# Attention totals spread by a transfer instead of GpSimd, and full tiles for the leftover rows of the last expert layer

## The reference

```
# L1 and L3 attention, per batch entry and head (L1: 4 heads, L3: 16), 1024 queries, 1024 + 154 keys, 64 wide
dots = jnp.einsum('bhid,bhjd->bhij', q, k) * scale
attn = jax.nn.softmax(dots, axis=-1)
out = jnp.einsum('bhij,bhjd->bhid', attn, v)
return out.transpose(0, 2, 1, 3).reshape(b, n, h * d) @ Wo + bo

# L3 experts: 2048 tokens, 32 experts, 4 per token, each expert takes at most cap = 320 tokens
xe = xp[buf_tok].reshape(E, cap, DIM)
h = jax.nn.silu(jnp.einsum('ecd,edh->ech', xe, w1)) * jnp.einsum('ecd,edh->ech', xe, w3)
out = jnp.einsum('ech,ehd->ecd', h, w2) * buf_w.reshape(E, cap, 1)
y = jnp.zeros((N + 1, DIM), x.dtype).at[buf_tok].add(out.reshape(E * cap, DIM))[:N]
```

## Time and profile before

| | |
|---|---|
| median of 3 runs | 3232.53 us (3228.24 to 3237.84) |
| the profiled execution's own time | 3235.65 us |
| its span | 3233.9 us |
| TensorE busy | 2877.3 us, 89% of the span |
| weight loads busy | 2129.0 us, 66% |
| VectorE busy | 1891.3 us, 58% |
| ScalarE busy | 1430.9 us, 44% |
| GpSimd busy | 658.2 us, 20% |

### The profile page before, as it was taken

One profiled execution on the slowest core, in us unless ns is written; L12 is line 12 of the kernel. 1 busy time (PEld: TensorE's weight loads), 2 busy tenths in 40 slices (PEclk: granted clock), 3 DMA queues, 4 the chain that ended last, 5 costly groups with the idle time before them and its releaser, 6 DMA issues. The chain is left out here.

```text
span 3233.9 us, 46916 instructions
## 1 busy us (share of the span) xinstructions
PE 2877.3 (89%) x14020; PEld 2129.0 (66%) x14021; DVE 1891.3 (58%) x3602; ACT 1430.9 (44%) x2987; POOL 658.2 (20%) x736
## 2 busy tenths in 40 slices
PE   6796789975998889999689999999999999579997
PEld 4795455534887678999556766766676666355664
DVE  4414465505555444434488888888888888273333
ACT  1232534431211115444447777777777777321110
POOL 0133001111442110000201111111111111106776
PEclk8797889995999779999799999999999999789999
DMA  1342010002322010000010101110100010036776
GB/s 40 122 150 86 2 27 15 15 1 90 101 95 92 15 40 27 26 13 0 17 29 17 23 15 30 22 23 15 23 21 17 23 24 8 1 70 159 164 159 140
DMA packets 147165, 158.11 MB, mean 49 GB/s; under 512 B 36816, under 2 KB 121702, under 8 KB 146726
## 3 DMA queue, kind: packets, MB, share of 16 engines
q1 hardware_dynamic: 109318, 94.41, 10.6%
q0 software_dynamic: 21280, 37.93, 5.4%
q10 hardware_dynamic: 16416, 24.12, 2.2%
HBM read 105.77 MB, written 29.84 MB: 42 GB/s over the span
## 5 line engine op out<-in xcount | busy, mean ns | idle before, releaser
L2035 ACT ACTIVATE l3a_pt_hi<-l3a_banks 128x512 fp32r<-128x512 f32 (+2 forms) x640 | 382.4, 598 | 314.3 <-PE l3a_banks L1976 257.0
L2146 DVE TENSOR_TENSOR l3a_pt_lo<-l3a_pt,l3a_pt_hi 128x512 fp32r<-128x512 f32 (+2 forms) x640 | 462.2, 728 | 81.0 <-ACT l3a_pt L2036 76.6
L2036 ACT ACTIVATE l3a_pt<-l3a_banks 128x512 f32<-128x512 f32 (+2 forms) x640 | 378.1, 591 | 0.0
L2116 DVE TENSOR_REDUCE l3a_maxima<-l3a_banks 128x1 f32<-128x1178 f32 x256 | 351.0, 1373 | 3.5 <-PE l3a_banks L1923 3.3
L1976 PE MATMUL l3a_banks<-l3a_pt_hi,l3a_v 128*65 128x512 f32 (+2 forms) x640 | 287.0, 448 | 12.1 <-ACT l3a_out L2050 12.1
L1989 PE MATMUL l3a_banks<-l3a_q,l3a_k 128*128 128x512 f32 (+2 forms) x640 | 254.5, 398 | 6.4 <-ACT l3a_pt L2036 4.9
L1990 PE MATMUL l3a_banks<-l3a_q,l3a_k 72*128 72x512 f32 (+5 forms) x640 | 253.5, 396 | 0.0
L1976 PE MATMUL l3a_banks<-l3a_pt_lo,l3a_v 128*65 128x512 f32 (+2 forms) x640 | 252.9, 395 | 0.0
L1976 PE MATMUL l3a_banks<-l3a_pt_hi,l3a_v_lo 128*65 128x512 f32 (+2 forms) x640 | 252.8, 395 | 0.0
L1923 PE MATMUL l3a_banks<-l3a_k,l3a_q 128*128 128x512 f32 (+1 forms) x768 | 207.8, 379 | 7.7 <-DVE l3a_maxima L2116 7.6
L2174 POOL PARTITION_BROADCAST l3a_shared<-l3a_inverse x65 | 62.6, 963 | 595.7 <-issue 595.7
(11 more groups left out here) (584 smaller groups left out, 6056.2 us busy)
## 6 DMA issues: line engine op xcount, KB each, us to landing
l3f_w<-in_L_ffn_w SPq DMA_DIRECT2D x96, 256.0 KB, 3.6
l0f_w<-in_L_ffn_W ACTq DMA_DIRECT2D x12, 1024.0 KB, 6.7
l1f_w<-in_L_ffn_W ACTq DMA_DIRECT2D x18, 512.0 KB, 4.5
l2f_w<-in_L_ffn_w SPq DMA_DIRECT2D x16, 512.0 KB, 4.6
l3a_q<-l3a_q SPq DMA_DIRECT2D x64, 128.0 KB, 2.3
l3a_k<-l3a_k SPq DMA_DIRECT2D x64, 128.0 KB, 2.3
l0f_w<-in_L_ffn_W SPq DMA_DIRECT2D x4, 1024.0 KB, 7.3
l1f_w<-in_L_ffn_W SPq DMA_DIRECT2D x6, 512.0 KB, 5.9
```

The lines of the kernel that those rows point to most:

```text
L2035: act.activation(a.pt_hi[0:rows, n % a.pt_slots, :], a.st_bank[0:rows, n % 2, :], ACT.Exp, bias=bias, scale=scale)
L2036: act.activation(a.pt[0:rows, n % 4, :], a.st_bank[0:rows, n % 2, :], ACT.Exp, bias=bias, scale=scale).then_inc(a.exped, 1)
L2116: dve.tensor_reduce(a.maxima[:, n:n + 1], banks.rearrange("p a b -> p (a b)")[:, 0:KEYS], AX.X, ALU.max).then_inc(a.maxed, 1)
L2146: dve.tensor_tensor(a.pt_lo[0:rows, slot, :], a.pt[0:rows, n % 4, :], a.pt_hi[0:rows, slot, :].bitcast(F32), ALU.subtract).then_inc(a.lo_m ...
```

## The change

1. In L1 and L3 attention `partition_broadcast` is gone. A third transfer of SP spreads the inverted row to 64 partitions, into a tile `shared` that has now two buffers, by the group's parity. GpSimd only multiplies. SP no longer waits for GpSimd's broadcast before it moves the inverses back, but waits until the spread has landed before it goes on.
2. In the L3 expert loop both rests of a pair are turned at once, as full 128 x 128 transposes, with the rows of the pair's first expert (6 transposes there, 4 for the second). `xt` holds a pair: columns 0 to 319 for the first expert, with its rest at the end, 320 to 639 for the second, with its rest at the start. The rest's product in `p_y` takes 72 columns of `hidden` instead of 64: the 8 added ones are spare zeros for the first expert, and columns of the next piece for the second; their results are not read.

```diff
 def move_totals(sp, a, k, g):
     sp.wait_ge(a.o_kept, k + 1)
     sp.dma_start(a.totals[:], a.out[HEAD:HEAD + 1, g % 2, :]).then_inc(a.moved, 16)
     sp.wait_ge(a.inverted, k + 1)
-    sp.wait_ge(a.spread_done, k + 1)
     sp.dma_start(a.inverse[:], a.totals[:]).then_inc(a.returned, 16)
     sp.wait_ge(a.returned, k * 16 + 16)
+    sp.dma_start(a.shared[:, g % 2, :], a.inverse[:].unsqueeze(1).to_broadcast([1, HEAD, BLOCK])).then_inc(a.spread_out[g % 2], 16)
+    sp.wait_ge(a.spread_out[g % 2], spread_count(k, g))
     sp.sem_inc(a.row_returned, 1)
...
     pool.wait_ge(a.ot_done, k + 2)
-    pool.wait_ge(a.returned, k * 16 + 16)
     pool.sem_inc(a.passed, 1)
-    pool.partition_broadcast(a.shared[0:HEAD, :], a.inverse[:], channels=HEAD).then_inc(a.spread_done, 1)
-    pool.wait_ge(a.spread_done, k + 2)
-    pool.sem_inc(a.passed, 1)
+    pool.wait_ge(a.spread_out[g % 2], spread_count(k, g))
     b, (hi, _) = g // 2, head_rows(g % 2)
-    pool.tensor_tensor(a.out_t[hi, parity, b * BLOCK:(b + 1) * BLOCK], a.out[0:HEAD, g % 2, :], a.shared[0:HEAD, :],
+    pool.tensor_tensor(a.out_t[hi, parity, b * BLOCK:(b + 1) * BLOCK], a.out[0:HEAD, g % 2, :], a.shared[:, g % 2, :],
                        ALU.mult).then_inc(a.ot_done, 1)
...
+    WIDE = REST + 8
+    IN_HIDDEN = ((0, P, 2 * P), (REST, REST + P, 0))
...
             def turn_rows(e, u, i):
                 pe.wait_ge(x_loaded[u], i * (16 * WHOLE) + 16 * WHOLE)
-                pe.wait_ge(rest_kept, i + 1)
-                pe.sem_inc(passed, 1)
+                if u == 0:
+                    pe.wait_ge(rest_kept, i + 1)
+                    pe.sem_inc(passed, 1)
                 pe.wait_ge(xt_kept, e * DC + 1)
-                rest = slice(u * REST, (u + 1) * REST)
                 for c in range(DC):
                     for j, (at, n) in enumerate(PIECES[0:WHOLE]):
-                        pe.transpose(p_xt[:, c, at:at + n], x_rows[:, u, j, c * P:(c + 1) * P], chip.ident[:])
-                    at, n = PIECES[WHOLE]
-                    ins = pe.transpose(p_xt[:, c, at:at + n], rest_tile[rest, c * P:(c + 1) * P], chip.ident[rest, rest])
+                        ins = pe.transpose(p_xt[:, c, at:at + n], x_rows[:, u, j, c * P:(c + 1) * P], chip.ident[:])
+                    if u == 0:
+                        ins = pe.transpose(p_xt[:, c, 2 * P:3 * P], rest_tile[:, c * P:(c + 1) * P], chip.ident[:])
                 ins.then_inc(x_turned, 1)
...
-                            ins = pe.matmul(p_h[:, k + f, 0:CAP], w[:, u, c, f * P:(f + 1) * P], xt[:, u, c, :],
+                            ins = pe.matmul(p_h[:, k + f, 0:CAP], w[:, u, c, f * P:(f + 1) * P], xt[:, c, u * CAP:(u + 1) * CAP],
                                             start=c == 0, stop=c == DC - 1)
...
-                    at, n = PIECES[j]
+                    at, n = IN_HIDDEN[u][j], P if j < WHOLE else WIDE
...
                 for c in range(DC):
-                    dve.tensor_copy(xt[:, u, c, :], p_xt[:, c, 0:CAP]).then_inc(xt_kept, 1)
+                    columns = slice(0, 3 * P) if u == 0 else slice(3 * P, 2 * CAP)
+                    dve.tensor_copy(xt[:, c, columns], p_xt[:, c, 0:columns.stop - columns.start]).then_inc(xt_kept, 1)
```

More of the change, by code:

```diff
@@ L1799, in __init__ @@
         self.inverse = sb("inverse", [1, BLOCK])
-        self.shared = sb("shared", [P, BLOCK])
+        self.shared = sb("shared", [HEAD, 2, BLOCK])
         self.out_t = sb("out_t", [P, 2, SEQ]) if out_t is None else out_t
@@ L1811, in __init__ @@
         self.inverted, self.returned, self.row_returned = sem("inverted"), sem("returned"), sem("row_returned")
-        self.spread_done, self.ot_done, self.passed = sem("spread_done"), sem("ot_done"), sem("passed")
+        self.ot_done, self.passed = sem("ot_done"), sem("passed")
+        self.spread_out = [sem("spread_out0"), sem("spread_out1")]
         self.passed_pe = sem("passed_pe")
@@ L2147, in attention_dve, with spread_count @@
                               ALU.subtract).then_inc(a.lo_made, 1)
+def spread_count(k, g):
+    return k * 8 + (8 + 8 * (g % 2))
 def move_totals(sp, a, k, g):
@@ L2598, in _ @@
                 pool.wait_ge(a.prepared, a.prepares)
-                pool.sem_inc(a.spread_done, 1)
                 pool.sem_inc(a.ot_done, 2)
@@ L2805, in l3_ffn @@
         z_silu, z_hidden = (chip.xn[:, n:n + 4, :].rearrange("p (f a) d -> p f (a d)", f=FC) for n in (0, 4))
-        x_rows, xt = sb("x_rows", [P, 2, WHOLE, ROW]), sb("xt", [P, 2, DC, CAP])
-        silu, hidden, y_rows = sb("silu", [P, FC, CAP]), sb("hidden", [P, FC, CAP]), sb("y_rows", [P, 2, 3, D])
+        x_rows, xt = sb("x_rows", [P, 2, WHOLE, ROW]), sb("xt", [P, DC, 2 * CAP])
+        silu, hidden, y_rows = sb("silu", [P, FC, CAP]), sb("hidden", [P, FC, CAP + 8]), sb("y_rows", [P, 2, 3, D])
         rest_flat = at_lane[:].bitcast(F32).rearrange("p n l -> p (n l)")[:, 0:PAIRS * ROW]
@@ L2825, in l3_ffn @@
         rest_indexed, rest_ready, rest_kept, passed = sem("rest_indexed"), sem("rest_ready"), sem("rest_kept"), sem("passed")
+        spare_cleared = sem("spare_cleared")
         block = stack.enter_context(nc.Block())
@@ L2871, in _ @@
             pool.sem_inc(y_free, 2)
+            pool.memset(hidden[:, :, CAP:CAP + 8], 0.0).then_inc(spare_cleared, 1)
             iota = dict(allow_small_or_imprecise_dtypes=True)
@@ L3037, in run @@
                         ins.then_inc(y_done, 1)
+            pe.wait_ge(spare_cleared, 1)
+            pe.sem_inc(passed, 1)
             pe.wait_ge(z_added, TILES // 2)
@@ L3074, in run @@
                 if more and u == 0:
-                    act.wait_ge(x_turned, e + 2)
                     act.wait_ge(rest_ready, i + 2)
@@ L3197, in run @@
                     dve.wait_ge(y_done, e * 3 + 1)
-                    dve.tensor_tensor(hidden[:, f, :], silu[:, f, :], p_h[:, 2 + f, 0:CAP], ALU.mult).then_inc(h_kept, 1)
+                    dve.tensor_tensor(hidden[:, f, 0:CAP], silu[:, f, :], p_h[:, 2 + f, 0:CAP], ALU.mult).then_inc(h_kept, 1)
                 if more or u == 0:
```

## The result

| | median, us | ratio to before (95% interval) |
|---|---|---|
| before, same chip | 3232.21 (3228.24 to 3237.84) | |
| after | 3201.97 (3198.12 to 3204.76) | 0.9905 (0.9893 to 0.9918) |

The change is worth 30 us where I forecast 76. The profiled execution took 3204.76 us (span 3203.0), against 3159.5 in my sum: 45 us are missing.

What follows compares the result with a forecast made beforehand. It took GpSimd's 15.2 us a group and TensorE's waits to bound attention's ends, TensorE the expert loop. Attention 56.2 plus experts 20 made 76 us: 3159.5 profiled, 3156.4 median, range 3143 to 3178.

Steps and rivals of the forecast that it cites:

- L3 attention, the end: From the last inverses' landing to TensorE's last projections in L3: without the broadcast 2814.2 against 2829.74, 15.5 us gained.
- L1 attention, the end: The same stretch at the end of L1 attention: 727.1 against 739.34, 12.2 us gained.
- the last unit's stops, and ScalarE's 7 us: Last units of L1 and L3: TensorE's stops and slow slots go, 21.5 us; ScalarE's waits for `out_t` go, 7 us.
- it fits by 0.4 us and costs nothing: SP, held 2.4 us longer per group, still lands L1's next totals before VectorE asks at 604.36: no loss.
- the expert layer, from L3's last projections to the program's end: L3 expert loop: GpSimd becomes the bound, 17.4 us over 28 experts, plus 2.7 for the last two: 20 us gained.
- The size of the spread: The new transfer of the inverted row to 64 partitions: taken as 2.3 us, allowed from 1.9 to 4.6.
- the spacing is wider: L3 attention: the next totals have more room behind the spread than in L1, as the reciprocal stands a slot later.
- the stop at slot 36: TensorE's wait for the second group in the last unit, 6.67 us in L1, 12.03 in L3: claimed to go.
- Slower, by the spread: Rival, chance 0.03: a spread over about 11 us delays totals to VectorE in all 20 units, 100 us; time over 3232.
- GpSimd's 15.2 us a group: Attention: broadcast, product and the idle before each cost GpSimd 6.0 + 0.8 + 7.1 + 1.25 us a group.
- the floor of 8.15 us: Expert loop: GpSimd's least time per expert, 7.85 us of work plus a 0.30 gap, against 8.77 before.
- the second rival: Expert loop gains nothing or little, as landings may get later or GpSimd's gap exceed 0.30: 3174, chance 0.16.

Runs made afterwards that it cites:

- expert_only: Only the last expert layer's part of the change, both attentions as in the kernel before: 3217.17 us, ratio 0.9941 to the kernel before.
- free_sp: Changed kernel, but SP does not stand still until the spread lands; it waits only before the next write of the inverse row: 3183.64 us, ratio 0.9840.
- g2_dram: As free_sp, but the inverse row of group 2, one of each unit's four, goes over DRAM: 3169.18 us, ratio 0.9800.
- no_weights: Changed kernel, but the last expert layer loads no weights inside its loop, so the output differs from the reference: 3192.10 us, ratio 0.9887.
- narrow_y: Changed kernel, but the rests' product in the last expert layer is 64 columns wide again, not 72; full-tile turning stays: 3217.08 us, ratio 0.9956.
- dram_source: Changed kernel, SP held as there, but the inverse row lies in DRAM and every spread reads it from there: 3160.57 us, ratio 0.9773.

## Why the prediction was wrong

Against the profiled execution my sum was 45.3 us too low. The terms:

| step, as the prediction put it | forecast | measured |
|---|---|---|
| L3 attention, the end | 15.5 | 11.7 |
| L1 attention, the end | 12.2 | 8.3 |
| the last unit's stops, and ScalarE's 7 us | 28.5 | 29.8 (9.4 + 20.4) |
| "it fits by 0.4 us and costs nothing" | 0 | -36.7 |
| the expert layer, from L3's last projections to the program's end | 20 | 14.3 |
| the rest of the program, untouched | 0 | 3.5 |
| sum | 76 | 31 |

The 3.5 us are scatter: from L1's last totals to L3's first it took 945.04 us before and 937.97 in expert_only, where nothing up to there is changed.

- **The size of the spread** is the root. I had the right doubt ("since all 64 reads come from one partition"), and gave it a bound of 4.6 us with nothing behind it. It is 6.3. At the two ends that cost 3.8 and 3.9 us, as it should: 6.3 less the 2.4 that I took. That much is a term mis-sized.
- **The step that failed** is "SP is held 2.4 us longer per group ... it fits by 0.4 us and costs nothing". With 6.3 us it does not fit. I named the waiter behind it and still priced it in L1 only, and put L3 aside with half a sentence ("the spacing is wider"). L3 has 16 of the 20 units and lost it all. free_sp shows 18 us of the 36.7 to be SP's hold, with the falls of the clock that hung on it.
- **What no step had**: the other half comes from spreads that keep the DMA engines busy when VectorE's loop jumps back and needs instructions. g2_dram shows that it is the length of the spread at that place, 14.4 us of the stretch by one spread in four; that it is instructions that come late rests on the silent instruction queue. Nor did any step have the half clock after each stop, some 8.5 us of the stretch, though the prediction priced it for the stop at slot 36.
- "Slower, by the spread" was the rival with the right mechanism for one half. I asked 11 us of it before it mattered and gave it 0.03. Its own formula gives at 6.3 us: 6.3 - 2.3 - 0.4 = 3.6 us at the tightest place of a unit. L1 has just that wait, after, in VectorE's timeline:

```profile
607.57 0.18 DVE L2172 RECIPROCAL l1a_totals<-l1a_totals 128x4 f32<-128x4 f32 x1 [3.47 <-DMA l1a_totals<-l1a_out]
```

  It stands there in three units, 3.37 to 3.53 us, and yet L1 loses nothing (from the first to the 16th totals 247.23 us before, 246.53 after). In L3 the waits are shorter, 1.7 us in the mean in 15 places, and TensorE loses by them. I take the difference to be VectorE's slack: before, it was busy 42% of 457 to 700 in L1, and 87% of the stretch in L3. So the formula gives a wait of VectorE, not a loss of time: taken over all 20 units it would say 72 us, four times what SP's hold cost.
- **Right**: GpSimd's 15.2 us a group vanish with the broadcast, and with them the stops at slot 36 and ScalarE's waits for `out_t`, of which the trace after has none left (29.8 us against 28.5). The recorded spans of GpSimd were no guide, as said. One source was misread without harm: the Trainium skill, DMA: Bandwidth & Descriptors, section "Anatomy of one DMA", gives its fixed cost for the transfers that GpSimd issues, and the spread is SP's.
- **The expert loop**: the floor of 8.15 us and the 20 us were right, and no_weights shows both; the 72 columns count as a full tile, and narrow_y shows that without them there is no gain. The miss of 5.7 us is what the second rival had named: landings get later as the loop tightens, and no_weights shows that they come early again without the weights' packets.

With the row in DRAM, the change does 3160.6 us, 41 us better than as it was made, and within 5 us of the forecast, with a spread 0.8 us longer than I had priced. That nearness is partly luck: its last units gave 32.0 us where I had 28.5, while its L3 stretch still lost 5.6 and its loop gave 5.4 less than the 20.

## What to carry to other kernels

A transfer that reads one partition many times is not priced by its bytes: here each read of 2 KB cost 0.075 us, so look at the source's layout before the size, and try a row that must be spread in DRAM (3.1 us here instead of 6.3). When a queue that waits for its own transfers gets a longer one, price the hold in every stage that has such a queue, in the stage with most rounds first, and not only at the place that looks tightest. Count what a stop of TensorE costs afterwards too: here 3.4 us at half the clock after each. Before moving a transfer that fills a wait, ask what then stands bare; here that cost 80 us.

## What the runs showed of the hardware

- 64 reads of 2 KB from one partition: 1.5 + 64 x 0.075 = 6.3 us; from 64 partitions 2.3, from DRAM 3.1.
- While a spread kept the 16 DMA engines 86.6% busy, no packet of the instruction queue moved for 4 us; the packets came when the spread had ended. VectorE stood some 6.2 us at the jump back of its loop, five times, and with a spread of 3.4 us there (g2_dram) not once. Before, its longest wait at the same instruction (`l3a_pt_lo`) was 2.8 us, for ScalarE.
- TensorE's granted clock fell to 0.50 for 3.4 us after stops of 0.97, 1.30 and 0.62 us in turn (after), and after one of 1.87 us (dram_source); after one of 0.80 us (before) and one of 1.68 us (g2_dram) it stayed at 1.00.
- A source with four rows outermost ran with 4 small packets instead of 16, and with 18.7 us of engine time instead of 60.3: 7.07 us.
